# Four moves in a four-layer graph network: VectorE's order in the attention and update steps, another bank for one W2 product, a value projection behind two scores, copies that start on part of their inputs

## The reference

```
layer 0:  agg = eps*h + adj @ h ;  u = silu(rmsnorm(agg @ W1 + b1) * w) ;  u @ W2 + b2         (W1 256x1024, W2 1024x256)
layer 1:  g = h @ W.T + b ;  att = sigmoid(g@a1 [i] + g@a2 [j] + c) * adj * mask*mask, rows normalised ;  (att @ g) * mask
layer 2:  8-head attention, head size 32, scores = q.k/sqrt(32) + adj * w_e[head], only where adj != 0 ; softmax ; @ v ; @ Wo.T
layer 3:  (D^-1/2 adj D^-1/2) @ (h @ W3) + b3
```

## Time and profile before

| | |
|---|---|
| time, median of 3 runs | 3776.06 us (3774.37 to 3779.08) |
| the profiled execution: its time, its span | 3772.78 us, 3771.0 us |
| granted clock of TensorE, mean | 0.996 |
| PE busy | 3599.3 us, 95% of the span |
| DVE busy | 2623.8 us, 70% |
| ACT busy | 2278.9 us, 60% |
| POOL busy | 771.7 us, 20% |
| DMA: the 4 copies a head into qk_stack | 1024, median 2.4 us from issue to landing |
| ACT's exponential of a score tile (L580) | mean 719 ns, 1024 of them |

### The profile page before, as it was taken

One profiled execution on the slowest core, in us unless ns is written; L12 is line 12 of the kernel. 1 busy time (PEld: TensorE's weight loads), 2 busy tenths in 40 slices (PEclk: granted clock), 3 DMA queues, 4 the chain that ended last, 5 costly groups with the idle time before them and its releaser, 6 DMA issues.

```text
span 3771.0 us, 67491 instructions
## 1 busy us (share of the span) xinstructions
PE 3599.3 (95%) x19596; PEld 2444.3 (65%) x19596; DVE 2623.8 (70%) x6436; ACT 2278.9 (60%) x5029; POOL 771.7 (20%) x1611
## 2 busy tenths in 40 slices
PE   6999999999999999999999999999999999999997
PEld 4666666666666666666666666666666666666664
DVE  5677677666776776776667767767766677677664
ACT  3665566655566655666555666656665556655564
POOL 1122221122221222211222212222112222122210
PEclk8999999999999999999999999999999999999999
DMA  2233223232232332232322323321323222233212
GB/s 97 51 90 84 70 59 79 67 89 67 67 78 57 88 84 72 57 81 65 89 67 67 78 60 85 85 71 56 85 61 89 68 69 76 65 80 88 63 46 67
DMA packets 166936, 275.09 MB, mean 73 GB/s; under 512 B 23906, under 2 KB 59874, under 8 KB 166756
## 3 DMA queue, kind: packets, MB, share of 16 engines
q1 hardware_dynamic: 166756, 273.45, 27.2%
HBM read 122.37 MB, written 16.78 MB: 37 GB/s over the span
## 4 chain that ended last, share of the span: by engine, by line
PE 61%; issue 13%; DVE 12%; POOL 8%; ACT 5%; POOLq 0%; SPq 0%; DMA 0%; DVEq 0%; ACTq 0%
PE turn L1217 9%; PE front L1030 6%; PE score L1207 6%; PE score L1208 6%; PE front L1031 6%; PE front L1032 6%; PE value L1232 3%; POOL small L373 3%; PE front L1083 3%; PE value L1193 3%; PE score L1181 3%; PE front L1060 3%; DVE pT L812 2%; ACT hf L492 2%; POOL x_out L439 2%
## 5 line engine op out<-in xcount | busy, mean ns | idle before, releaser
L580 ACT ACTIVATE prob<-prob,small 128x512 f32<-128x512 f32 x1024 | 736.1, 719 | 375.0 <-DVE small L887 373.4
L887 DVE CUSTOM_DVE_ANT_0 prob<-score,adj_sb,drv 128x512 f32<-128x512 f32 x1024 | 759.7, 747 | 223.7 <-PE score L1208 214.2
L1217 PE MATMUL turn<-ident,prob 128*128 128x128 f32 x4096 | 614.5, 275 | 15.1 <-ACT pT L589 8.5
L1217 PEld LDWEIGHTS turn<-ident,prob 128*128 128x128 f32 x4096 | 482.4, 141 | 135.4 <-issue 61.6
L589 ACT ACTIVATE pT<-turn 128x512 f32<-128x512 f32 x768 | 446.7, 584 | 143.5 <-PE turn L1217 143.5
L1207 PE MATMUL score<-qk_stack 128*128 128x512 f32 x1024 | 495.0, 487 | 32.0 <-DVE small L887 30.1
L1208 PE MATMUL score<-unlinked,neg_mask 128*128 128x512 bf16 x1024 | 398.9, 390 | 0.0
L1030 PE MATMUL front<-w_hi,s_hi 128*128 128x256 f32 x1024 | 354.3, 346 | 34.7 <-DVE x_in L791 28.6
L678 DVE TENSOR_TENSOR s_lo<-front,s_hi 128x512 fp32r<-128x512 f32 x320 | 217.8, 681 | 104.9 <-ACT s_hi L485 104.8
L1031 PE MATMUL front<-w_lo,s_hi 128*128 128x256 f32 x1024 | 289.1, 282 | 0.0
L1032 PE MATMUL front<-w_hi,s_lo 128*128 128x256 f32 x1024 | 288.7, 282 | 0.0
(11 more groups left out here) (160 smaller groups left out, 7450.4 us busy)
## 6 DMA issues: line engine op xcount, KB each, us to landing
qk_stack<-qk SPq DMA_DIRECT2D x1024, 128.0 KB, 2.4
adjT_f<-in_adjT SPq DMA_DIRECT2D x32, 1024.0 KB, 5.3
adj_sb<-in_adj SPq DMA_DIRECT2D x32, 1024.0 KB, 7.9
prob<-in_adjT SPq DMA_DIRECT2D x32, 1024.0 KB, 5.3
x_new<-in_x SPq DMA_DIRECT2D x32, 512.0 KB, 3.9
out<-x_out SPq DMA_DIRECT2D x32, 512.0 KB, 3.2
pT<-in_W SPq DMA_DIRECT2D x2, 1024.0 KB, 11.6
rmsw_b<-in_rmsw SPq DMA_DIRECT2D x1, 512.0 KB
```

The costliest lines, as they stand in the source:

```text
L580: act.activation(prob[:, i % 8, :], prob[:, i % 8, :], ACT.Exp, bias=nmax[:, h, n:n + 1], scale=-1.0, accum_out=prsum[:, h, n:n + 1]).then ...
L887: dve.tensor_tensor_reduce(out=prob[:, i % 8, :], in0=SB_[i % 2][:, :], in1=adj_sb[:, n, :], scale=neg_w[:, h:h + 1], scalar=3e38, op0=ALU ...
L1217: last = pe.transpose(TB[k % 2][:, tile(n)], prob[:, (4 * h + n) % 8, tile(j)], ident[:, :])
```

## The change

Five edits:

1. `stack`: the four copies of a head are issued in another order (q high with k high, q low with k high, q high with k low, q low with k low), and for heads 0 and 4 SP waits ahead of the first only for the high parts, ahead of the second for the low part of q, ahead of the last two for the low part of k.
2. `project_v(t, 1)` on PE goes from ahead of the grid to step g = -2, behind scores 0 and 1 and ahead of score 2; its copy `values(t, 1)` on ACT goes behind exponential 1.
3. On DVE the updates (with their statistics) are issued behind the other steps of the same grid step, so that the low part of tile n+1 comes ahead of update n.
4. The last tile's W2 product goes into FB[0] in place of FB[2], and doesn't wait for the update of tile 2 any more.
5. `logits` is split: the four s1 instructions, then `attended(t, 1)`, then the four s2 instructions. Each of the eight writes a slot of `hid` that a row tile has to itself; the s2 one waits for the s1 one of its tile.

```diff
--- before.py
+++ after.py
@@ -218,6 +218,10 @@
         GRID = range(-4, 4 * H)
         Q1_STEP, K1_STEP = 0, 3
 
+        def down_bank(n):
+
+            return FB[0 if n == NT - 1 else 2][:, 0:D]
+
         def linear_bank(n):
 
             return (FB[0], FB[2], FB[1], FB[0])[n][:, 0:D]
@@ -268,15 +272,26 @@
                 elif later(t):
                     sp.wait_ge(sc_ps, at(t, 32, 0))
                     unregistered(sp)
+                def part(c, q, k):
+                    sp.dma_start(qk_stack[HD * c:HD * c + HD, s, :, :].bitcast(F32),
+                                 qk[r, q:k + 1:k - q, :].bitcast(F32)).then_inc(stacked[s], 16)
+
                 if h % HG == 0:
 
                     sp.wait_ge(qk_hi_ready, at(t, 4, 2 * g + 2))
                     unregistered(sp)
+                part(0, 0, 2)
+                if h % HG == 0:
+
+                    sp.wait_ge(qk_lo_ready, at(t, 4, 2 * g + 1))
+                    unregistered(sp)
+                part(2, 1, 2)
+                if h % HG == 0:
+
                     sp.wait_ge(qk_lo_ready, at(t, 4, 2 * g + 2))
                     unregistered(sp)
-                for c, (q, k) in enumerate(((0, 2), (0, 3), (1, 2), (1, 3))):
-                    sp.dma_start(qk_stack[HD * c:HD * c + HD, s, :, :].bitcast(F32),
-                                 qk[r, q:k + 1:k - q, :].bitcast(F32)).then_inc(stacked[s], 16)
+                part(1, 0, 3)
+                part(3, 1, 3)
 
             def back2(t):
                 for h in range(H):
@@ -603,8 +618,6 @@
                     values(t, 0)
                 if f:
                     square(tf, 0, 1)
-                if b:
-                    values(t, 1)
                 for g in GRID:
                     if f:
                         for n, u in tile_steps(g):
@@ -616,6 +629,8 @@
                                 hidden_hi(tf, n, u - 6)
                     if b and g + 4 < 4 * H:
                         exps(t, g + 4)
+                    if b and g == -3:
+                        values(t, 1)
                     if b and g >= 0 and g % 4 != DVE_TURN:
                         turned_probs(t, g // 4, g % 4)
                     if b and g == Q1_STEP + 1:
@@ -788,22 +803,26 @@
                 if n == 0:
                     dve.wait_ge(b2_added, at(tf, 1, 1))
                 dve.wait_ge(down_ps, at(tf, 16, 4 * n + 4))
-                dve.tensor_tensor(x_in[:, n, :], FB[2][:, 0:D], x_in[:, n, :], ALU.add).then_inc(x0_ready, 1)
-
-            def logits(tf):
+                dve.tensor_tensor(x_in[:, n, :], down_bank(n), x_in[:, n, :], ALU.add).then_inc(x0_ready, 1)
+
+            def logits1(tf):
                 if later(tf):
 
                     dve.wait_ge(s1_ps, at(tf, 1, 0))
                     dve.wait_ge(sig_ready, at(tf, 4, 0))
                 for n in range(NT):
                     dve.wait_ge(f_norm["ready"], at(tf, 8, 4 + n + 1))
-                    if n >= 2:
-                        dve.wait_ge(s2_ready, at(tf, 4, n - 1))
-                        dve.wait_ge(s1_ready, at(tf, 4, n - 1))
-                    for c, dst, init, ready in ((0, s2, s_const, s2_ready), (1, s1, 0.0, s1_ready)):
-                        dve.tensor_tensor_reduce(out=hid[:, N * (n % 2) + D * c:N * (n % 2) + D * c + D], in0=hf[:, n, :], in1=wa[:, c, :],
-                                                 scale=1.0, scalar=init, op0=ALU.mult, op1=ALU.add,
-                                                 accum_out=dst[:, n:n + 1]).then_inc(ready, 1)
+                    dve.tensor_tensor_reduce(out=hid[:, D * n:D * n + D], in0=hf[:, n, :], in1=wa[:, 1, :],
+                                             scale=1.0, scalar=0.0, op0=ALU.mult, op1=ALU.add,
+                                             accum_out=s1[:, n:n + 1]).then_inc(s1_ready, 1)
+
+            def logits2(tf):
+                for n in range(NT):
+
+                    dve.wait_ge(s1_ready, at(tf, 4, n + 1))
+                    dve.tensor_tensor_reduce(out=hid[:, D * n:D * n + D], in0=hf[:, n, :], in1=wa[:, 0, :],
+                                             scale=1.0, scalar=s_const, op0=ALU.mult, op1=ALU.add,
+                                             accum_out=s2[:, n:n + 1]).then_inc(s2_ready, 1)
 
             def attention1(tf):
                 dve.wait_ge(mask_loaded, at(tf, 16, 16))
@@ -952,7 +971,8 @@
                                 silu(tf, n, u - 4)
                             elif u in (6, 7):
                                 hidden_lo(tf, n, u - 6)
-                            elif u == (9 if n == NT - 1 else 15):
+                        for n, u in tile_steps(g):
+                            if u == (9 if n == NT - 1 else 15):
                                 update0(tf, n)
                                 stats(tf, 1, f_norm, norm_tiles(0), x_in, n)
                     if prepare is not None and g == 3:
@@ -975,10 +995,11 @@
                 if b:
                     inverse_out(t, 1)
                 if f:
-                    logits(tf)
+                    logits1(tf)
                 if b:
                     attended(t, 1)
                 if f:
+                    logits2(tf)
                     attention1(tf)
                 if b:
                     update2(t)
@@ -1088,13 +1109,13 @@
                 c = q // 2
                 pe.wait_ge(s_hi_ready, at(tf, 8, 2 * n + c + 1))
                 pe.wait_ge(s_lo_ready, at(tf, 8, 2 * n + c + 1))
-                if q == 0 and n:
+                if q == 0 and 0 < n < NT - 1:
                     pe.wait_ge(x0_ready, at(tf, 4, n))
                 elif q == 0 and later(tf):
 
                     pe.wait_ge(msg_ready, at(tf, 4, 0))
                 for f in range(2 * q, 2 * q + 2):
-                    last = product(FB[2][:, 0:D], (s_hi[:, f, :], s_lo[:, f, :]), (w2_hi[:, f, :], w2_lo[:, f, :]),
+                    last = product(down_bank(n), (s_hi[:, f, :], s_lo[:, f, :]), (w2_hi[:, f, :], w2_lo[:, f, :]),
                                    f == 0, f == FT - 1)
                 last.then_inc(down_ps, 1)
 
@@ -1287,8 +1308,6 @@
                     project_v(t, 0)
                 if f:
                     hidden(tf, 0, 1)
-                if b:
-                    project_v(t, 1)
                 if shared is not None:
                     shared()
                 for g in GRID:
@@ -1306,6 +1325,8 @@
                                 turn_hidden(tf, n, u - 5)
                             for q in quarters(n, u):
                                 down(tf, n, q)
+                    if b and g == -2:
+                        project_v(t, 1)
                     if b and g < 0:
                         scores(t, g + 4)
                     if b and g == Q1_STEP:
```

## The result

The changed kernel takes 3734.12 us (median of 4 runs, 3728.87 to 3734.47) against 3776.75 for the kernel before in the same session: ratio 0.9885, 95% interval 0.9872 to 0.9897. The forecast was 3736.5 us. The profiled execution has a span of 3732.7 us, forecast 3731.5.

The account below looks back on a forecast made before the run. PE is busy 95% of the span, so its waits are nearly all there is to win. Savings of 32 x 0.2 + 32 x 0.85 + 31 x 0.19 = 39.5 us took the median 3776.06 to 3736.5 us; range 3714 to 3755.

Parts of the forecast that it names:

- First scores: Start of the score tiles on PE: values fill idle time, copies issued earlier gate score 0; 0.2 us a graph.
- Rival (b): First scores: the copies are no gate, so 0.7 us a graph is gained, 3720.5 us; chance 8%.
- (c): First scores: copies land where they did and PE waits for them, -0.6 us a graph, 3762 us; chance 8%.
- (e): First scores: copies land so late that the kernel is slower, -1.4 us a graph, 3788 us; chance 4%.
- Last W2 product: Last tile's W2 product on PE: its wait for the update of x goes, low part just in time; 0.85 us a graph.
- the sign of being wrong here: Last W2 product: PE still standing more than 0.2 us ahead of or inside it would refute the forecast.
- Rival (d): Last W2 product: the wait for x is only handed on to the low part, 0.43 us, 3750 us; chance 6%.
- Edit 5: Attended rows between the logits: PE reaches the output projection 0.91 us earlier, but only 0.19 us a pass is gained.
- at the fourth, 3 x 0.43 on: In attend1, PE reaches the fourth product at 1808.96 and must wait for the fourth attention product until 1809.68.
- the signs that I gave for being wrong here: Attended rows between the logits: no wait for line 812 appears, and the period falls below 113.4 us.
- the next gate: Normed rows of layer 3: last one at 1817.05, PE wants it at about 1817.55, so 0.19 us passes.
- Rival (a): Third attention product: DVE gets ahead of POOL, it takes 0.75 us, the full 0.91 comes through, 3714 us; chance 12%.

Follow-up runs that it names:

- the bank alone: The kernel before with only the last tile's W2 product moved to FB[0], DVE's order as it was: 3767.15 us, ratio 0.9971.

## Why the prediction was right, and where it wasn't

**First scores: right in mechanism, a little too large in size.** The copies are the new gate, with score 0 at 8.97 us (forecast 8.90), and score 4 hangs on the bias of score 2 (forecast and seen). The term was 0.2 us, measured 0.15 at score 4 in the changed kernel and 0.11 a pass alone. Rival (b) falls with the 0.40 us of waiting, and rivals (c) and (e) aren't this kernel, but what edit 2 would be without edit 1: there the forecast's -0.6 us was -0.75 measured.

**Last W2 product: right in mechanism and nearly in size, with two slips that nearly cancel.** 0.85 taken, 0.76 in the changed kernel and 0.72 alone. I let the product start at 1792.61, the modelled end of the turn. In the changed kernel it starts 0.36 us behind the turn's start; that distance in the earlier trace rows gives 1792.37, which is 1.14 us ahead of 1793.51 and not 0.90. But then the second half is wanted 0.24 us earlier too, before the low part is there, and PE stands 0.29 us inside the product instead of finding it just in time. That is over the 0.2 us that I had given as the sign of being wrong here; by the idle time of the profile, 0.15 us, it isn't. The bound for the case without edit 3, 0.43 us less, was measured at 0.46. Rival (d) is the bank alone, which gave 0.26 where (d) had 0.43.

**Edit 5: the step that failed is "at the fourth, 3 x 0.43 on".** The attention products do end when I said, and PE does come 0.9 us earlier. But I read a row of L1115 (now L1136) as one product of the code. The page of the changed kernel (group, then busy us and mean ns, then idle time before):

```profile
L1136 PE MATMUL front<-pT,hf 128*128 128x512 f32 x512 | 228.1, 599 | 2.0 <-DVE pT L831 2.0
```

That is 16 for each of 32 graphs, and the code issues 8 (2 halves of the features, 4 row tiles): each float32 product of 512 columns stands in the trace as two rows. The text ahead of the prediction has the same slip where it speaks of 16 matmuls there and of 8 in each half of the values (the code issues 4). So PE wants the fourth attention product 6 x 0.43 = 2.6 us behind the first, not 1.3; it had 1.5 us of slack before and has 0.7 after. Of the signs that I gave for being wrong here, the first came (no wait for these products) and the second didn't (the period is 113.72, not below 113.4). What stops the gain is what I had as "the next gate", the normed rows of layer 3: PE comes to aggregate3 1.48 us earlier than before (the row at 1798.11 against the earlier trace rows), of which 0.91 from the two other places, and 0.57 from this one, because 0.32 of the 0.89 us it had at attend1 go in front of aggregate3. I had let 0.19 us pass this gate by the last of the four normed rows, and again with 0.43 us a product. The first one decides: before, it was written at 1815.58 (the first of the four instructions in the earlier trace rows takes 0.60 us), 0.67 us ahead of PE at 1816.25, and edit 5 doesn't bring it forward (ACT's row of four starts 93.03 us into the pass before and 92.08 after, 0.95 less, of which the two other places have 0.91). At the end of the pass 0.49 is left. In the trace DVE's update chain there starts right behind its work on the diagonal, with no pause for PE, where it paused 0.28 us before; that this takes the last 0.1 us is argued, not tested. The term was 0.19, measured 0.46 alone and 0.49 in the changed kernel. Rival (a) had the right place for what is still missing: with POOL's sums out of the way 0.32 us more comes through.

**The sum** of a pass was 1.24 us against 1.40: the first two terms 0.14 too high, the third 0.3 too low. That the span came within 1.2 us of the forecast is in part luck, since in these two executions the start and the last pass took 6 us of the difference back; by the medians 42.6 us were saved where 39.5 were forecast. The parts alone add up to 0.11 + 0.72 + 0.46 = 1.29 us, the whole has 1.40; the 0.1 between them I leave open.

## What to carry to other kernels

Work that is moved to fill an idle stretch may itself have been the cover of a transfer: find what lands behind it, and move only as much as the transfer doesn't need. When a wait on a bank is taken away, look at once for what the same instructions wait for next, and at the order in which the engine that owes it works; here the bank alone gave a third. Count how many rows of a trace one instruction of the code makes before spacing its inputs by them. Reckon when PE gets to an instruction from the distance of starts, not from the modelled end of the matmul ahead. Where several instructions each wait for their own input, look at the slack of the first, too, and not of the last alone.

## What the runs showed of the hardware

**A product of two SBUF operands on VectorE beside a sum on GpSimd takes 1.74 us instead of 0.75.** The line of the attention products over all 128, in the changed kernel and with POOL's sums behind them (min, median, max in ns):

```profile
L831 DVE SCALAR_TENSOR_TENSOR pT<-pT,mask_sb,adjT_f x128: 736/744/1744, 84.2 to 3610.8; 128x512 f32<-128x512 f32 x128
```
```profile
L831 DVE SCALAR_TENSOR_TENSOR pT<-pT,mask_sb,adjT_f x128: 742/745/752, 82.7 to 3598.9; 128x512 f32<-128x512 f32 x128
```

POOL's first sum starts 0.07 us ahead of the third product and ends 0.55 us before that product does; taking the sum away takes the whole 1 us away. The other way round it is POOL that gets slower: its second sum starts 0.24 us behind the fourth product (1791.51 against 1791.27) and takes 1.63 us, where it takes 1.27 with no product beside it. POOL's sums in the changed kernel, then with all of them behind the products:

```profile
L445 POOL TENSOR_TENSOR pT<-pT x96: 1263/1269/1717, 85.7 to 3612.8; 128x512 f32<-128x512 f32 x96
```
```profile
L445 POOL TENSOR_TENSOR pT<-pT x96: 1264/1268/1278, 85.7 to 3602.6; 128x512 f32<-128x512 f32 x96
```

The Trainium skill (SBUF — State Buffer, Who interferes with whom) calls the ports that the two share an exclusive lock and says that the order of issue decides who blocks. The trace agrees on who gives way, in both orders. If the lock were held for the whole sum, the product would end 0.75 us behind it; it ends 0.55 behind.

**One plain float32 product of the code stands in the trace as two rows, a float32r product or a transpose as one.** For each graph the code issues 8 products on L1136 (512 columns), 8 on L1214 (256 columns) and 32 on L1228 (float32r, which the view prints as f32). The trace has 16, 16 and 32 rows; the four transposes of L1127 are 4 rows.

```profile
L1214 PE MATMUL value<-ws,bT x512: 377/379/634, 118.1 to 3650.5; 128*128 128x256 f32 x171
L1228 PE MATMUL score<-qk_stack x1024: 467/481/987, 122.0 to 3696.9; 128*128 128x512 f32 x171
L1127 PE MATMUL front<-ident,small x128: 272/273/476, 81.1 to 3605.5; 128*128 128x128 f32 x128
```

**The granted clock at both ends of the program differs from trace to trace, for the same instructions.** In the changed kernel's profiled execution PE stood 3.5 us for the copies in the last pass, and its clock was at half (1.2 GHz) in the 6 us of the first window below. With the same wait in the kernel with edits 1 and 2 alone it stayed at 2.4 GHz. The windows, changed kernel, then that one (busy us of PE, weight loads, DVE, ACT and POOL, granted clock, share and GB/s of DMA):

```profile
3645.00:3651.00 6.00, 5.38 (x13) 3.71 (x13) 1.68 (x5) 1.63 (x4) 1.21 (x2) 0.50 0.91 198
```
```profile
3684.60:3690.60 6.00, 5.37 (x21) 3.31 (x22) 3.56 (x10) 3.52 (x9) 0.82 (x1) 1.00 0.92 199
```

The three kernels with edit 4, edits 3 and 4, or edit 5 alone run the same instructions in their last pass as the kernel before, since in a pass without a front half these edits change nothing. They took 95.3 to 95.6 us for it, against 93.06. A window of the one with edit 4 alone, where the same stretch of the kernel before has a clock of 1.00:

```profile
3683.40:3689.40 6.00, 5.78 (x10) 2.30 (x10) 2.28 (x6) 3.26 (x10) 0.00 (x0) 0.50 0.75 167
```

Likewise the kernel with edits 1 and 2 alone has the instructions of the kernel before in its first stretch, and took 112.93 us for it against 110.08. So a difference of 2 to 3 us at either end, as between the two traces of this case, comes without any change, and the medians (42.6 us apart) show next to none of it. What makes the clock fall in one trace and not in the other these runs don't show.
